# A restack of attention queries: block-major instead of token-interleaved

## The reference, cut to what matters

```python
q = (x @ Wq + bq).reshape(B, S, H, hd).transpose(0, 2, 1, 3)      # H = 16, hd = 8, S = 2048
k = (x @ Wk + bk) ...; v = (x @ Wv + bv) ...
scores = jnp.einsum('bhqd,bhkd->bhqk', q, k) * scale
allowed = (j <= i) & (i - j < WINDOW)                             # WINDOW = 32
attn = softmax(where(allowed, scores, NEG_INF)); out = attn @ v
x = x + out @ Wo + bo
x = x + ffn(layernorm(x))                                         # 128 -> 512 -> 128
```

## Time and profile before

| | before |
|---|---|
| median of three runs | 165.35 us |
| span of the profiled execution | 162.8 us |
| TensorE busy, matmuls | 145.1 us, 89% |
| VectorE, ScalarE, GpSimd busy | 61%, 55%, 31% |
| DMA queue q1, share of the 16 DMA engines | 43.0% |

### The profile page before, as it was taken

How to read it: one execution, slowest core, us unless ns; L and a number is a source line. 1 busy time by engine, 2 the same in 40 slices (tenths; PEclk the granted TensorE clock), 3 DMA queues, 4 the chain that set the end, 5 groups by cost and what they waited for, 6 DMA issues and landing times.

```text
span 162.8 us, 5053 instructions
## 1 busy us (share of the span) xinstructions
PE 145.1 (89%) x1923; PEld 113.8 (70%) x1923; DVE 99.5 (61%) x281; ACT 89.3 (55%) x256; POOL 51.0 (31%) x78
## 2 busy tenths in 40 slices
PE   0755298699999999999999999999799999999993
PEld 0423185578887887888788878788667665958792
DVE  6687956945576685695595597869665354221021
ACT  3354357558386577666677757529912567060600
POOL 6369578910060060051041030503600039800000
PEclk9999999659999999999999999999999999999999
DMA  1786897957044928618809908900000000020213
GB/s 50 219 215 243 202 366 168 330 168 178 0 151 167 240 97 268 188 61 297 195 4 332 212 0 306 230 19 0 4 0 4 0 2 4 0 64 0 64 45 88
DMA packets 27313, 21.10 MB, mean 130 GB/s; under 512 B 1304, under 2 KB 23071, under 8 KB 27295
## 3 DMA queue, kind: packets, MB, share of 16 engines
q1 hardware_dynamic: 27294, 20.85, 43.0%
HBM read 10.88 MB, written 9.96 MB: 128 GB/s over the span
## 4 chain that ended last, share of the span: by engine, by line
PE 80%; ACT 7%; DVE 5%; issue 2%; SPq 2%; DMA 1%; POOL 1%; DVEq 0%
PE bank_o L490 20%; PE bank_s L458 16%; PE bank_s L469 9%; PE bank_qk L611 4%; PE bank_s L513 4%; PE bank_w L536 3%; PE bank_v L611 3%; PE bank_o L513 3%; PE bank_qk L422 3%; ACT V L628 3%; PE bank_v L428 3%; PE bank_w L532 2%; PE bank_qk L423 2%; PE bank_t L416 2%; DMA x_sb<-in_L_attn_x_dram 1%
## 5 line engine op out<-in xcount | busy, mean ns | idle before, releaser
L490 PEld LDWEIGHTS bank_o<-V,probsT 128*32 128x32 f32 x1024 | 33.1, 114 | 15.1 <-issue 14.2
L458 PEld LDWEIGHTS bank_s<-KS,QS 128*128 128x128 bf16 x512 | 35.6, 166 | 4.5 <-ACT probs L684 3.9
L458 PE MATMUL bank_s<-KS,QS 128*128 128x64 bf16 x512 | 35.8, 225 | 2.3 <-ACT probs L684 2.2
L490 PE MATMUL bank_o<-V,probsT 128*32 128x36 f32 x1024 | 36.8, 201 | 0.0
L827 DVE TENSOR_REDUCE negmax<-bank_s 128x8 f32<-128x512 f32 x32 | 22.1, 690 | 22.9 <-PE bank_s L458 21.5
L684 ACT ACTIVATE probs<-bank_s 128x512 f32<-128x512 f32 x32 | 19.1, 598 | 22.4 <-PE bank_s L469 22.3
L628 ACT ACTIVATE V<-bank_v 32x64 f32<-32x64 f32 x128 | 27.5, 215 | 1.5
L840 DVE STREAM_TRANSPOSE probsT<-probs 128x512 f32<-128x512 f32 x32 | 22.5, 702 | 0.0
L285 POOL TENSOR_TENSOR q_parts<-rest,q_parts 128x256 bf16<-128x256 f32 x8 | 5.6, 705 | 53.7 <-ACT q_parts L628 53.7
L372 POOL TENSOR_TENSOR rstd<-var,half 128x4 f32<-128x4 f32 x4 | 4.1, 1020 | 28.6 <-DVE var L871 28.6
L469 PE MATMUL bank_s<-negmax,ident_bf 128*128 128x512 bf16 x32 | 12.6, 395 | 0.1
(11 more groups left out here) (109 smaller groups left out, 232.5 us busy)
## 6 DMA issues: line engine op xcount, KB each, us to landing
k_scr<-k_parts SPq DMA_DIRECT2D x8, 576.0 KB, 5.0
KS<-k_scr SPq DMA_DIRECT2D x8, 576.0 KB, 5.1
q_scr<-q_parts SPq DMA_DIRECT2D x8, 512.0 KB, 3.0
QS<-q_scr SPq DMA_DIRECT2D x32, 128.0 KB, 3.0
x_sb<-in_L_attn_x_dram SPq DMA_DIRECT2D x1, 768.0 KB, 5.3
out_dram<-y SPq DMA_DIRECT2D x3, 256.0 KB, 2.3
w<-in_L_ffn_W_dram SPq DMA_DIRECT2D x2, 256.0 KB, 5.4
x_sb<-in_L_attn_x_dram SPq DMA_DIRECT2D x2, 128.0 KB, 2.2
```

The costliest lines, as they stand in the source:

```text
L458: mm = nc.tensor.matmul(dst, QS[b][:, o, g].rearrange("p h t -> p (h t)")[:, j::BLOCKS], KS[b][:, o, g, j * WIN:(j + 2) * WIN], start=(i = ...
L490: mm = nc.tensor.matmul(o[q * WIN:(q + 1) * WIN, g * VC:(g + 1) * VC], probsT[s % 2][:, i, g, w, :], V[b][:, j + w, g, :], start=(w == 0), ...
```

## The change

What it does:

- `QS` becomes [partition, o, g, block, head, query]. The 128 columns of one score product are one contiguous run (L458 of before).
- The token order of the query parts is natural: `by_query` goes, in `high`, in `split_rest` and in the masks' slots (`set_one_hot`, `mask_slots`).
- The query scratch becomes [head column of the group, part, (o, g), token]. Its write is no longer one DMA per chunk but eight, one for each slot, with 256 tokens (512 bytes) a run. `q_in` then counts 8 x 16.
- The four reads into `QS` have the same bytes, but where a run was 256 tokens it is now 32 queries of one block (64 bytes), because a head's blocks no longer lie side by side in `QS`.
- `set_q`, which fills the one-hot half of `QS`, is four copies instead of one.

```diff
-        QS = two("QS", [P, 2, NG, GH, CHUNK], BF16)
+        QS = two("QS", [P, 2, NG, BLOCKS, GH, WIN], BF16)
...
-        q_scr, k_scr = (
-            [nc.dram_tensor(f"{n}_scr{i}", (2 * NG, GH * HD, SLOTS // 2, width), BF16).ap() for i in range(2)]
-            for n, width in (("q", CHUNK), ("k", KW)))
+        q_scr = [nc.dram_tensor(f"q_scr{i}", (GH * HD, SLOTS // 2, 2 * NG, CHUNK), BF16).ap() for i in range(2)]
+        k_scr = [nc.dram_tensor(f"k_scr{i}", (2 * NG, GH * HD, SLOTS // 2, KW), BF16).ap() for i in range(2)]
+        Q_WRITES = SLOTS * 16
...
-                for low, scr, slots, done in ((low_q_done, q_scr[b], q_parts[b], q_in[b]),
-                                              (low_done, k_scr[b], k_parts[b], k_in[b])):
-                    sp.wait_ge(low, c + 1)
-                    sp.dma_start(scr.rearrange("(o g) r c t -> (g r) o (c t)", o=2),
-                                 slots[:].rearrange("p (o c) t -> p o (c t)", o=2)).then_inc(done, 16)
+                sp.wait_ge(low_q_done, c + 1)
+                for o in range(2):
+                    for part in range(SLOTS // 2):
+
+                        sp.dma_start(q_scr[b][:, part, o * NG:(o + 1) * NG].rearrange("r g t -> g r t"),
+                                     q_parts[b][:, o * SLOTS // 2 + part]).then_inc(q_in[b], 16)
+                sp.wait_ge(low_done, c + 1)
+                sp.dma_start(k_scr[b].rearrange("(o g) r c t -> (g r) o (c t)", o=2),
+                             k_parts[b][:].rearrange("p (o c) t -> p o (c t)", o=2)).then_inc(k_in[b], 16)
...
-                sp.wait_ge(q_in[b], 16 * turn + 16)
+                sp.wait_ge(q_in[b], Q_WRITES * turn + Q_WRITES)
                 for hh in range(GH):
 
-                    sp.dma_start(QS[b][hh * WIN:(hh + 1) * WIN].rearrange("p o g h t -> p (o g) h t")[:, :, hh, :],
-                                 q_scr[b].rearrange("n (h r) c t -> h (r c) n t", h=GH)[hh]).then_inc(stacked[b], 16)
+                    sp.dma_start(QS[b][hh * WIN:(hh + 1) * WIN].rearrange("p o g n h q -> p (o g n) h q")[:, :, hh, :],
+                                 q_scr[b].rearrange("(h r) c m (n q) -> h (r c) (m n) q", h=GH, q=WIN)[hh]
+                                 ).then_inc(stacked[b], 16)
...
-                            mm = nc.tensor.matmul(dst, QS[b][:, o, g].rearrange("p h t -> p (h t)")[:, j::BLOCKS],
+                            mm = nc.tensor.matmul(dst, QS[b][:, o, g, j].rearrange("p h q -> p (h q)"),
...
-                ident_act(q_parts[b][:, 2].rearrange("p (q n) -> p q n", q=WIN), by_query(bank_qk), bias=bqc)
+                ident_act(q_parts[b][:, 2], bank_qk[:, 0:CHUNK], bias=bqc)
...
-                nc.vector.tensor_copy(QS[b][:, 1].rearrange("p g h t -> p (g h) t"),
-                                      one_hot[:].unsqueeze(1).to_broadcast([P, NG * GH, CHUNK])).then_inc(q_set, 1)
+                for g in range(NG):
+                    nc.vector.tensor_copy(QS[b][:, 1, g],
+                                          one_hot[:].rearrange("p (n q) -> p n q", q=WIN).unsqueeze(2).to_broadcast(
+                                              [P, BLOCKS, GH, WIN])).then_inc(q_set, 1)
```

More of the change, by code:

```diff
@@ L178, in ge @@
                 eng.wait_ge(s, value)
-        def by_query(bank_):
-            return bank_[:, 0:CHUNK].rearrange("p (n q) -> p q n", q=WIN)
         def high_half(t):
@@ L233, in restack @@
                 sp.wait_ge(repeat_done, c + 1)
-                for low, scr, slots, done in ((low_q_done, q_scr[b], q_parts[b], q_in[b]),
-                                              (low_done, k_scr[b], k_parts[b], k_in[b])):
-                    sp.wait_ge(low, c + 1)
-                    sp.dma_start(scr.rearrange("(o g) r c t -> (g r) o (c t)", o=2),
-                                 slots[:].rearrange("p (o c) t -> p o (c t)", o=2)).then_inc(done, 16)
+                sp.wait_ge(low_q_done, c + 1)
[6 more added lines that the diff above has]
+                             k_parts[b][:].rearrange("p (o c) t -> p o (c t)", o=2)).then_inc(k_in[b], 16)
                 if isinstance(turn, int) and turn == 0:
-                    sp.wait_ge(q_set, 2 + b)
+                    sp.wait_ge(q_set, 1 + NG * (b + 1))
                     if b == 1:
@@ L342, in _ @@
             ln1_rstd(3, 2 * TILES, 4 * TILES)
-            nc.gpsimd.memset(QS[1][:, 0].rearrange("p g h t -> p (g h t)").bitcast(U32), 0).then_inc(zeroed_pool, 1)
+            nc.gpsimd.memset(QS[1][:, 0].rearrange("p g n h q -> p (g n h q)").bitcast(U32), 0).then_inc(zeroed_pool, 1)
             low_parts(0, 1)
@@ L434, in mask_slots @@
                 pe.wait_ge(consts, 8)
-                one_hot_cols = ident_bf[0:2 * WIN, 0:2 * WIN].rearrange("p (e q) -> p q e", e=2).unsqueeze(2)
+                one_hot_cols = ident_bf[0:2 * WIN, 0:2 * WIN].rearrange("p (e q) -> p e q", e=2).unsqueeze(1)
                 band_cols = band[:].unsqueeze(1)
@@ L438, in mask_slots @@
                     pick_rows = select[:, s].rearrange("p g r -> p (g r)")
-                    nc.tensor.matmul(bank_o[0][:, s * CHUNK:(s + 1) * CHUNK].rearrange("p (q n e) -> p q n e", q=WIN, e=2),
-                                     pick_rows, one_hot_cols.to_broadcast([2 * WIN, WIN, BLOCKS // 2, 2]),
+                    nc.tensor.matmul(bank_o[0][:, s * CHUNK:(s + 1) * CHUNK].rearrange("p (n e q) -> p n e q", q=WIN, e=2),
+                                     pick_rows, one_hot_cols.to_broadcast([2 * WIN, BLOCKS // 2, 2, WIN]),
                                      start=True, stop=True)
@@ L638, in high @@
                 if not (isinstance(turn, int) and turn == 0):
-                    act.wait_ge(q_in[b], 16 * turn)
+                    act.wait_ge(q_in[b], Q_WRITES * turn)
                     act.wait_ge(k_in[b], 16 * turn)
                 ge(act, repeat_done, c)
-                ident_act(q_parts[b][:, 2].rearrange("p (q n) -> p q n", q=WIN), by_query(bank_qk), bias=bqc)
+                ident_act(q_parts[b][:, 2], bank_qk[:, 0:CHUNK], bias=bqc)
                 ident_act(k_parts[b][:, 1, WIN:], bank_qk[:, CHUNK:], bias=bkc).then_inc(high_done, 1)
@@ L775, in set_one_hot @@
                 for s in range(2):
[L776 to L779, removed]
+                    cols = one_hot[:].rearrange("p (n e q s) -> p s n e q", s=2, n=BLOCKS // 2, e=2)[:, s]
+                    rows = ident_bf[:].rearrange("p (e q c) -> p c e q", e=2, c=SLOTS // 2)[:, 2 + s]
+                    nc.vector.tensor_copy(cols, rows.unsqueeze(1).to_broadcast(
+                        [P, BLOCKS // 2, 2, WIN // 2])).then_inc(one_hot_set, 1)
             def set_q(b):
-                nc.vector.tensor_copy(QS[b][:, 1].rearrange("p g h t -> p (g h) t"),
-                                      one_hot[:].unsqueeze(1).to_broadcast([P, NG * GH, CHUNK])).then_inc(q_set, 1)
+                for g in range(NG):
+                    nc.vector.tensor_copy(QS[b][:, 1, g],
+                                          one_hot[:].rearrange("p (n q) -> p n q", q=WIN).unsqueeze(2).to_broadcast(
+                                              [P, BLOCKS, GH, WIN])).then_inc(q_set, 1)
             def ln1_var(t0, t1):
@@ L806, in split_rest @@
                 ge(dve, low_done, c)
-                nc.vector.scalar_tensor_tensor(rest[:, 0].rearrange("p (q n) -> p q n", q=WIN), by_query(bank_qk), bqc,
-                                               q_parts[b][:, 2].rearrange("p (q n) -> p q n", q=WIN),
+                nc.vector.scalar_tensor_tensor(rest[:, 0], bank_qk[:, 0:CHUNK], bqc, q_parts[b][:, 2],
                                                ALU.add, ALU.subtract)
@@ L893, in update_weights @@
                                                ALU.add).then_inc(weff_done, 1)
-            nc.vector.memset(QS[0][:, 0].rearrange("p g h t -> p (g h t)").bitcast(U32), 0).then_inc(q_set, 1)
+            nc.vector.memset(QS[0][:, 0].rearrange("p g n h q -> p (g n h q)").bitcast(U32), 0).then_inc(q_set, 1)
             dve.wait_ge(x_first, 16)
```

## The result

The changed kernel takes 207.92 us (median of five runs, 207.29 to 209.79), the kernel before 165.35 us beside it: a ratio of 1.261, 95% interval 1.254 to 1.268. The forecast was 203 us, range 175 to 240. The profiled span is 208.0 us, 45.2 more than before. The profiled execution is the slowest of the five (209.79 us); the one that gives the median has a span of 206.2 us. Three executions of the experiments (two with both transfers cheap, one with eight writes into the old scratch and contiguous columns) ran in a slower state at a lower granted clock, and differences that involve these two kernels leave them out.

A forecast was written before the change was run, and what follows sets the result against it. TensorE bounds the kernel before; afterwards the DMA queue, at 16.7 us a chunk, starts chunk 7 at 147.9 instead of 111.14, + 36.8. Span 162.8 + 37 = 200, and 2.55 from span to median gives 203 us, range 175 to 240.

The forecast's parts named there:

- The bound moved from TensorE to the DMA queue: Steady chunks: TensorE set the pace at 12.70 us; after the change the queue would, at 16.7 us where TensorE needs 11.0.
- 2.7 us of slack: Restack of chunk 4: lands at 70.5 us and is needed at 73.17, so a longer delay would show.
- What the scores gain: Score products on TensorE: contiguous queries take each from 59 to 33 ns, 13.3 us in all, 1.7 a chunk.
- The writes on four engines: Query scratch writes: eight DMAs on the same four engines, 256 runs of 29 ns each, 7.4 us a chunk.
- k = 4: Number of engines a DMA with a slowest dimension of 4 uses, counted from completion packets in the profile before.
- The reads of 64-byte runs: Query reads into QS: 512 runs an engine at 11.4 ns, 5.8 us a chunk instead of 1.9.
- the rival of dear runs: Query reads: runs near 29 ns, reads 14.8 us, time about 275; at 20 ns, 239; chance 0.20.
- The estimate of 15 ns a run: Query reads: unaligned 64-byte runs fetch 5 beats instead of 2, 7.7 us a chunk, about 15 us on the forecast.
- The sum: Queue per chunk: query write 7.4, landing to first read 1.5, reads 5.8, KS 2.0, together 16.7 us.
- The 2.55 us between span and time: Whole kernel: the profiled span lay 2.55 us below the median of the runs, taking span 200 to time 203.
- The rival of spread writes: Query writes use more engines and cost their issue time, + 2.7 us; chunks 13.4 us each, about 177 us; chance 0.15.
- The copies and the token order: Dropping by_query changes nothing; set_q as four copies delays chunk 0 by 0.3 us, left in the rounding.

The follow-up runs named there:

- both transfers cheap: Changed kernel with its query writes on sixteen engines and its query reads in 512-byte runs (bytes of QS misplaced): 170.15 us, ratio 1.034 to the kernel before.
- the column edit: Kernel before with one line changed: score products take 128 contiguous columns of QS, transfers untouched, scores of other queries: 151.97 us, ratio 0.921.
- the interleaved one: Kernel before with tokens interleaved by four in half-chunks, column step 4, eight query reads of 256-byte runs, one query write, right output: 157.94 us, ratio 0.955.

## Why the prediction was right, step by step

**The bound moved from TensorE to the DMA queue: right.** It rested on 2.7 us of slack; every run that lengthened the restack by more lost, and the size of the loss followed the restack. The 2.7 is chunk 4's; chunks 5 to 7 had 4.0 to 4.2 by the same reckoning. From its first write to the landing of `KS`, the restack of chunk 6 took 9.9 us before, 12.5 with eight writes into the old scratch, and 18.1 with writes on sixteen engines and 21.1 in the changed kernel (these two up to the first scores, which wait for it); the times are 165, 167, 189 and 208 us.

**What the scores gain: right.** 13.3 us forecast from 33 ns a product; the column edit alone gave 12.8. The product is even 29 ns at full clock. In the changed kernel nothing of it shows at the end.

**The writes on four engines: right in kind, and the largest inference of the text.** The count of completions carried it: 7 for four small DMAs led to k = 4 for the slowest dimension of 4; the packets came out to the unit, here and on sixteen engines. That they are the same four is shown by the share of 0.30 in the write stretch; eight DMAs spread over different engines would have shown much more. The Trainium skill's rule (DMA: Bandwidth & Descriptors, Why a DMA increments its semaphore by 16 and not by 1) holds on this. The size was forecast at 7.4 us a chunk and is 6.2: runs were priced with their overlap left out.

**The reads of 64-byte runs: the size right, the mechanism not, and that is luck.** The forecast took 11.4 ns a run on the engines, 5.8 us a chunk; the phase took 6.3, and the records give 10.8 ns a run. But the engines can pass a run every 7 ns, 3.6 us for 512 (an estimate from the 145 GB/s at the peak of each read), and run nearly dry between the reads. What takes 6.3 us is SyncE's queue, about 1.55 for each of the four. The forecast had this mechanism only as a word in the rival of dear runs ("the DMA queue must also make the descriptors") and gave it no price: the issue time of the reads stands in none of its sums. The estimate of 15 ns a run from the Trainium skill (DMA: Bandwidth & Descriptors, How a descriptor splits into AXI transactions) is not borne out: it would hold a read phase at 7.7 us at least, and at the peak a run takes half of it.

**The sum.** Forecast 2.0 + 7.4 + 1.5 + 5.8 = 16.7 us a chunk, measured 3.0 + 6.2 + 1.7 + 6.3 = 17.2 in the stretch shown and 17.5 on average. The term that was most too small is `KS`, priced at full rate with nothing for its start: in the stretch shown it moves about 100 GB/s until 119 us and about 300 only after. The write's error, in the other direction, hid that. Chunk 0 starts at 33.46 instead of 31.0 and chunk 7 at 156.14 instead of 147.9. Behind it are 51.9 us, forecast 51.7. The span of the profiled execution is so 8 us above the 200 of the sum, and that of the median execution 6 us, while the time is 5 above the 203. The 2.55 us between span and time was the distance of a median from another execution's span; in one and the same execution the two lie 1.7 to 1.8 us apart.

**The rival of spread writes was mis-sized.** It gave 177 us; the run was 188.7. One step that failed is the issue time, taken as 0.38 us a DMA from a row in which each issue followed a pause. Back to back it is 0.43, and with the new scratch 0.6; the kernel's own reads issued back to back, 0.45, would have been a better price. So the restack was 18.1 us instead of 16.6 (chunk 6, from 104.13 to the scores at 122.28). The other is the way from the scores of a chunk to the first write two chunks on, 11.8 us (92.31 to 104.13) instead of 10.1. The scores of chunk 4 had waited 3.8 us, and the 32 value products behind them read 1.91 us where they read 1.12 at full clock: the loop itself goes through the cold clock.

**The copies and the token order** cost nothing that shows: the four copies of `set_q` take 2.49 and 1.91 us for the two buffers, where the one copy took 1.22 in one and 1.72 in the other, and the first write of chunk 0 starts at 12.71 us, before at 12.78.

Where the 43 us come from: the columns give back 13, and the restack costs more than four times as much. Taken back in turn from 207.9: small runs and four engines together about 39 (29.5 and 19.2 when each is taken back alone; the two don't add, since another limit takes over), the new scratch with what goes with it about 10, the number of writes about 7; that leads to the 152.0 of the column edit.

## What to carry to other kernels

Before a layout is changed for one engine's sake, write down for each DMA on the way the length of a run, the slowest dimension of both sides, the number of issues and the number of runs in each, and hold the sum against the slack of the transfer. A strided operand need not become contiguous: try the step between (here 4 of 8), which can give most of the gain and keep runs long. And count completions in a trace: they tell how many engines a DMA shape really uses.

## What the runs showed of the hardware

- A 128-column bf16 weight load with 64 moving columns: 29 ns a product at column steps of 1 and 2 elements, 34 at 4, 59 at 8, at the 2.4 GHz level.
- Four reads of 2,048 runs of 64 bytes, issued back to back, held SyncE's queue for about 1.55 us each behind the first, and the 16 DMA engines ran nearly dry between them (5 or 6 GB/s against 145 at the peak, a run every 7 ns on an engine). Reads of 256 runs, of 512 bytes in the kernel before and of 256 in the interleaved one, took 0.45 to 0.49 in most chunks.
- DMAs whose destination had a slowest dimension of 4 left 4 completion packets each (90,910 packets in all), and a stretch of them alone had a DMA share of 0.30.
- TensorE's granted clock fell from 1.00 to 0.50 (1.2 GHz) in the waits of the changed kernel: in the one before chunk 5 TensorE stood idle from 117.7 to 121.5 us, and the clock was 0.57 in 119.5 to 120 us, then 0.50, and 1.00 again from 126.5. Between the chunks this cost nothing, since the transfers set the pace. Behind the last wait it shows: the third score group of chunk 7 starts 8.1 us after the first, where it was 6.8 with strided columns.
- The issue of one DMA with 128 to 256 runs took 0.43 to 0.48 us or about 0.6 us in kernels whose DMAs were alike in number and bytes. They differed in the scratch layout, the cut of the writes, the shape of `QS` and the token order; the cut is not the cause. Open.
